# Moving router tables, a first transposition and a gate group within one core's instruction order (decoder layer with mixture of experts, Trainium2)

## The reference, cut to what matters

```
x = x + attention(layernorm(x))                       # 16 heads of 16
x = x + mlstm(q=layernorm(x), k=v=ctx, gates)         # 8 heads of 32
x = x + moe(layernorm(x))                             # 8 experts, 2 taken per token

# gates of the mlstm, for all tokens
pre  = 15 * tanh((concat(q, k, v) @ ifgate_w.T + b) / 15)
lf   = cumsum(log_sigmoid(f_pre)); running maximum m; d = exp(...)
den  = max(|sum|, exp(-m)) + 5e-5
# router
probs = softmax(x @ router_w + router_b); top 2 of 8
out  += weight(e) * (gelu(x @ up[e].T) @ down[e].T)   # for each chosen e
```

## Time and profile before

| what | value |
|---|---|
| time, median of 3 runs | 1005.02 us (1004.59 to 1009.46) |
| the profiled execution: its own time | 1006.74 us |
| its span, first to last instruction | 1005.0 us |
| what lies around the span | 1.74 us |
| PE, DVE, ACT, POOL busy | 89%, 61%, 48%, 52% |
| mean granted TensorE clock | 0.947 of full |
| second stage, about | 339 to 571 us |
| overlap of second and third stage, about | 571 to 640 us |
| tiles alone, about | 640 to 1003 us |

### The profile page before, as it was taken

The page is one execution under the profiler, slowest core; times in us unless marked ns, Lnnn a source line. Parts: engine busy times, 40 slices in busy tenths (PEclk is TensorE's granted clock), DMA queues, the critical chain, the costliest instruction groups (busy, mean ns, idle before and its releaser), DMA issues.

```text
span 1005.0 us, 31744 instructions
## 1 busy us (share of the span) xinstructions
PE 894.1 (89%) x11966; PEld 662.6 (66%) x11966; DVE 614.9 (61%) x1340; ACT 484.4 (48%) x810; POOL 526.7 (52%) x660
## 2 busy tenths in 40 slices
PE   4798898989897777789989798999999999999995
PEld 3566666766665445566666486787787878787783
DVE  4766767777666434777778657555555555555553
ACT  3556766766666445555555444233333333333331
POOL 2545655655655333467878767644434443444342
PEclk8999999999998778798989789999999999999998
DMA  9112343234234654245555324343333332333322
GB/s 282 55 26 73 79 105 114 76 86 135 77 85 128 134 155 139 86 143 172 173 169 174 111 61 91 78 92 49 49 50 50 50 49 46 53 46 53 50 29 27
DMA packets 133198, 92.97 MB, mean 93 GB/s; under 512 B 75712, under 2 KB 114112, under 8 KB 132928
## 3 DMA queue, kind: packets, MB, share of 16 engines
q1 hardware_dynamic: 119760, 73.10, 26.5%
q0 software_dynamic: 13296, 17.83, 10.7%
HBM read 54.65 MB, written 37.32 MB: 92 GB/s over the span
## 4 chain that ended last, share of the span: by engine, by line
PE 59%; DVE 12%; ACT 7%; POOL 6%; DMA 5%; issue 4%; SPq 2%; POOLq 0%; DVEq 0%; ACTq 0%
PE pair L950 19%; PE pair L964 11%; PE pair L966 6%; POOL sm L1567 3%; PE pair L679 3%; PE pair L665 3%; PE pair L643 3%; DMA o_scr<-On 2%; PE pair L692 2%; DMA STG<-wup_in 2%; PE pair L821 1%; PE pair L916 1%; DVE SD L1146 1%; ACT xn L1319 1%; PE pair L835 1%
## 5 line engine op out<-in xcount | busy, mean ns | idle before, releaser
L950 PE MATMUL pair<-XTs,WU 128*128 128x128 bf16 x3408 | 287.2, 221 | 10.2 <-DVE XTs L1287 4.5
L950 PEld LDWEIGHTS pair<-XTs,WU 128*128 x3408 | 240.9, 99 | 77.8 <-issue 15.0
L1604 POOL DMA_INDIRECT out_d<-XB x71 | 115.4, 1626 | 208.4 <-DVE XB L1309 178.9
L964 PE MATMUL pair<-WD,Hh 128*128 x568 | 215.5, 380 | 0.0
L1480 ACT ACTIVATE Hf<-pair 128x512 f32<-128x512 f32 x142 | 84.9, 598 | 227.1 <-PE pair L950 227.1
L1300 DVE CAST Hh<-Hf 128x512 bf16<-128x512 f32 x142 | 63.0, 444 | 173.1 <-ACT Hf L1480 171.7
L966 PE MATMUL pair<-WD,Hl 128*128 x568 | 155.1, 273 | 0.0
L1525 POOL TENSOR_SCALAR_AFFINE_SELECT PT<-PT 128x512 f32<-128x512 f32 (+1 forms) x96 | 74.7, 792 | 61.4 <-ACT PT L1338 55.2
L1302 DVE TENSOR_TENSOR Hl<-Hf,Hh 128x512 bf16<-128x512 f32 x142 | 99.8, 703 | 4.9
L1036 DVE TENSOR_REDUCE mxn<-pair 128x4 f32<-128x1024 f32 x64 | 75.2, 1216 | 25.9 <-PE pair L624 25.9
L1146 DVE TENSOR_TENSOR SD<-pair,SD 128x1024 f32<-128x1024 f32 x48 | 58.6, 1221 | 40.8 <-ACT SD L1422 33.3
(11 more groups left out here) (241 smaller groups left out, 1807.7 us busy)
## 6 DMA issues: line engine op xcount, KB each, us to landing
XB<-xs_scr SPq DMA_DIRECT2D x71, 130.0 KB, 2.1
STG<-wup_in SPq DMA_DIRECT2D x32, 256.0 KB, 4.9
q_scr<-SPL SPq DMA_DIRECT2D x16, 512.0 KB, 4.0
STG<-wdn_in SPq DMA_DIRECT2D x32, 256.0 KB, 2.9
o_scr<-On SPq DMA_DIRECT2D x32, 128.0 KB, 4.1
Mm<-o_scr SPq DMA_DIRECT2D x16, 256.0 KB, 3.0
CnT<-ctxt_in SPq DMA_DIRECT2D x16, 256.0 KB, 4.7
CX<-ctx_in SPq DMA_DIRECT2D x16, 256.0 KB, 4.0
```

The lines of the kernel that those rows point to most:

```text
L950: t = e.matmul(upb(j, k)[:, 128 * (fm % 4):128 * (fm % 4) + 128], WU[:, bass.ds(reg[j] * 4096 + off, 128)], XTs[:, r, hx, dk, :], start=n ...
L964: e.matmul(yb[r][:, 0:512], Hh[:, r, hsl], WD[:, bass.ds(reg[i] * 4096 + 512 * fk, 512)], start=fk == 0, stop=False, skip_group_check=True)
L1604: e.indirect_dma_start(out=out, out_offset=bass.IndirectOffsetOnAxis(ap=XS[:, i % NX, 256:257].bitcast(I32), axis=0), in_=Yf[:, i % NY, :] ...
```

## The change

Three things are done, all in the order of steps. No instruction is added or dropped on any engine.

First, in `rest`, GE of the second gate group goes from (4, 0) to (4, 2), Gp from (4, 1) to (5, 0) and Go from (4, 2) to (5, 1).

Second, in `tail`, part -1 is taken out of the first block of five and put ahead of the last PV (batch 15, unit 2); parts 0 to 3 stay where they are.

Third, around the last pair's router steps: R2 comes after part 40 (before: 41), R3 after part 41 (before: 41), R4 after part 46 (before: 44), R5 and R6 after part 50 (before: 48). The tables no longer follow R6 in one piece: they are cut in three, after parts 52, 54 and 56. The whole overlap gets four more parts.

```
-            (3, 0): (("GA", z), ("Gt", 1)), (3, 1): (("GT", 1),), (3, 2): (("Gs", 1),), (4, 0): (("GE", 1),), (4, 1): (("Gp", 1),),
-            (4, 2): (("Go", 1),)}
+            (3, 0): (("GA", z), ("Gt", 1)), (3, 1): (("GT", 1),), (3, 2): (("Gs", 1),), (4, 2): (("GE", 1),), (5, 0): (("Gp", 1),),
+            (5, 1): (("Go", 1),)}
...
-    tail = (("PV", z, 1), ("B4x", a), ("R6", z - 4), ("PV", z, 2), ("B3", z), ("B4o", a), ("B5s", a), ("B5", z - 2), ("experts", 5),
+    tail = (("PV", z, 1), ("B4x", a), ("R6", z - 4), ("experts", 1), ("PV", z, 2), ("B3", z), ("B4o", a), ("B5s", a), ("B5", z - 2), ("experts", 4),
...
-            ("B6", z), ("experts", 4), ("R1", z), ("experts", 6), ("R2", z), ("R3", z), ("experts", 3), ("R4", z), ("experts", 4),
-            ("R5", z), ("R6", z), ("tables", 0), ("experts", 17))
+            ("B6", z), ("experts", 4), ("R1", z), ("experts", 5), ("R2", z), ("experts", 1), ("R3", z), ("experts", 5),
+            ("R4", z), ("experts", 4), ("R5", z), ("R6", z), ("experts", 2), ("tables", 0), ("experts", 2), ("tables", 1), ("experts", 2),
+            ("tables", 2), ("experts", 13))
...
+        def vector_tables(e, w, link, n):
+            if n == 0:      # L1261 to L1269 of before
...
+            elif n == 1:    # L1270 to L1276
...
+            else:           # L1277 to L1281
```

More of the change, by code:

```diff
@@ L1221, in vector_mlstm @@
                 elif kind == "tables":
-                    vector_tables(e, w, link)
+                    vector_tables(e, w, link, b)
                 elif kind == "R6":
@@ new lines, in vector_tables @@
+        def vector_tables(e, w, link, n):
+            if n == 0:
+                e.tensor_copy(cni[:, :], CNT).then_inc(t_ci, 1)
+                link(e.tensor_tensor(t8[:, 1, :], CNT, CF[:, C_RB:C_RB + 8], ALU.subtract))
+                e.tensor_copy(t8[:, 5, :], PMe[:, :])
+                link(e.tensor_scalar(t8i[:, :], t8[:, 1, :], 63.5, 1.0 / 128.0, ALU.add, ALU.mult))
+                e.tensor_copy(t8[:, 2, :], t8i[:, :])
+                link(e.tensor_tensor(t8[:, 5, 1:8], PMe[:, 1:8], PMe[:, 0:7], ALU.subtract))
+                e.tensor_scalar(t8[:, 6, :], t8[:, 5, :], -128.0, None, ALU.mult)
+                link(e.tensor_tensor(t8[:, 2, :], t8[:, 2, :], t8[:, 5, :], ALU.subtract))
+                e.scalar_tensor_tensor(t8[:, 6, 0:7], t8[:, 5, 1:8], 128.0, t8[:, 6, 0:7], ALU.mult, ALU.add)
+            elif n == 1:
+                e.tensor_tensor_scan(t8[:, 4, :], t8[:, 2, :], t8[:, 2, :], 0.0, ALU.add, ALU.max)
+                link(e.tensor_scalar(t8[:, 3, :], t8[:, 2, :], -128.0, float(REG), ALU.mult, ALU.add))
+                e.tensor_scalar(t8[:, 7, :], t8[:, 5, :], 128.0, None, ALU.mult)
+                link(e.tensor_tensor(te8[:, :, :], over(t8[:, 4, :], NF), tile_nos(0, NF), ALU.is_le))
+                e.tensor_tensor(t8[:, 3, :], t8[:, 3, :], t8[:, 6, :], ALU.add)
+                link(e.tensor_reduce(TE[:, :], te8[:, :, :], AX.X, ALU.add))
+                e.tensor_scalar(TE[:, :], TE[:, :], 7.0, None, ALU.min)
+            else:
+                link(e.tensor_tensor(te8[:, :, :], te8[:, :, :], over(t8[:, 3, :], NF), ALU.mult))
+                e.tensor_copy(TEi[:, :], TE[:, :])
+                link(e.tensor_reduce(RB[:, :], te8[:, :, :], AX.X, ALU.add))
+                link(e.scalar_tensor_tensor(RB[:, :], CF[:, C_J:C_J + NF], 128.0, RB[:, :], ALU.mult, ALU.add))
+                e.tensor_scalar(RBi[:, :], RB[:, :], t8[:, 7, 0:1], None, ALU.add).then_inc(t_rb, 1)
```

22 lines of the change are left out of this document (removed).

## The result

The changed kernel took 1001.41 us (median of 7 runs, 1000.63 to 1004.4), the kernel before in the same comparison 1007.1 us (median of 7, which include the three of the table above). The ratio is 0.9947, 95% interval 0.9927 to 0.9966: 0.5% faster, within what I had forecast (1000.2 us, range 996.9 to 1003.6). The profiled execution took 1000.63 us with a span of 998.9 us, against 1006.74 and 1005.0.

A forecast was written before the change was run, and what follows sets the result against it. PE was taken as the bound, busy 89% of the span. The three edits, -0.4 + 1.1 + 4.1 = 4.8 us, came off the 1005.0 us median for 1000.2 us, range 996.9 to 1003.6.

The forecast's parts named there:

- First edit, -0.4 us: Gate group moved: PE's 3 us lead ends waiting for R3's result; 0.4 us lost, bounds 1.5 us either way.
- the replay: Forecast's step-by-step timing of the new order; at the gate group, the product of (5, 1) starts at 428.9, against 428.83.
- 0.4 us loss: Price put on a possible slow clock behind PE's new gap of nearly 2 us ahead of the scores of (5, 2).
- Gp takes the lead back: Gate group on DVE: Gp's 3.0 us ahead of the product of (5, 1) uses up batch 3's power coming about 3 us sooner.
- Second edit, +1.1 us: Part -1 ahead of the last PV: part 0 starts at 574.7 instead of 575.80; 1.1 us gained, bounds 0.3 to 2.8.
- the bound on the clock: Parts 0 to 3: an earlier start may end the slow clock stretch sooner, for up to 1.7 us more.
- rival C: Gate group gains what its gap promises, or slow stretch after part 0 ends sooner: 1.5 or 1.7 us more; chance 0.2.
- Third edit, +4.1 us: Router steps and tables: wait moves from part 56 to 64, which starts at 633.85 against 637.94; bounds 1.8 to 5.4 us.
- rival B: Clock falls in the gap ahead of part 64 or at (5, 2): 3.0 us gained, 1002.0 us; chance 0.28.
- Rival D: Table work and Gp on DVE held up beside POOL: four steps hit lose 2.4 us, 1002.6 us; chance 0.07.
- this stays: Ahead of part 0, PE still needs 1.29 us after low(0) for the register load and what follows it.
- its 1.3 us is exposed: At part 64 the register load, unseen before, stands behind the wait for low(8) and now costs 1.3 us.

The follow-up runs named there:

- e10: The change with Gp and Go both at (5, 2), behind the product of (5, 1): 1012.11 us, ratio to before 0.9935.
- e1: The kernel before with only the gate group (GE, Gp, Go) moved to its new places: 1010.67 us, ratio to before 1.0019.
- e3: The kernel before with only the last pair's router steps and the three table pieces placed as in the change: 1006.22 us, ratio 0.9979.
- e5: The change itself, measured again in a later comparison: 1014.86 us, ratio to before 0.9972.
- e2: The kernel before with only part -1 put ahead of the last PV: 1005.57 us, ratio to before 0.9963.
- e4: The change with the gate group back in its old places: 998.24 us, ratio to before 0.9911.
- e6: The change with the second and third table pieces each a tile later: 1015.97 us, ratio to before 0.9976.
- e7: The change with the load of the expert numbers put ahead of PE's wait for low(j): 1008.80 us, ratio to before 0.9902.
- e9: The kernel before with only the load of the expert numbers put ahead of PE's wait: 1014.97 us, ratio to before 0.9962.

## Why the prediction was right, and where it was not

The time forecast, 4.8 us saved, met the 5.3 us of the ratio (0.53% of 1007), but two of its terms were wrong by 2 to 4 us in opposite directions. That the sum fits is luck as much as insight: the interval of the ratio alone allows 3.4 to 7.4 us. By its own steps:

**First edit, -0.4 us.** The chain on DVE held: no wait at L757 (0.6 us in the forecast), 1.99 us of idle time ahead of the scores of (5, 2), the product of (5, 1) at P + 24.1 us where the replay had P + 24.8, because B4x came 0.7 us sooner than replayed. R4 followed 0.6 us sooner instead of at the same time. What was too small is the price of the clock behind the gap, "0.4 us loss": the lower level lasted 10 us, in all five kernels with this order, which turned the 0.6 us into 0.8 us lost at P + 51 us. The term comes out near its 0.4 because the two misses oppose each other. The argument that Gp takes the lead back is what e10 tested: with Gp behind the product, the gap and the slow stretch are gone and P to R is 3.5 us shorter.

**Second edit, +1.1 us.** The step itself was exact: V to U is 1.2 us shorter, and from the end of low(0) to part 0 it took 575.24 - 574.02 = 1.22 us (1.29 in the forecast). What failed is the bound on the clock: "an earlier start may end that stretch sooner, for up to 1.7 us more" was half of rival C at a chance of 0.2. It came in every kernel with the second edit, and beside before, e1 and e3 it is worth 3.4 to 4.8 us. I had priced the slow stretch by parts 0 to 3 alone, the 24 matmuls of the earlier trace rows and one row, and never looked for its end. The rows of before that I had not read show it at 0.50 from 576 to 587 us. At half speed over 11 us that is a much larger stake than 2.74 us of matmuls. Why the stretch ends sooner with this edit stays open.

**Third edit, +4.1 us.** The wait moved from part 56 to part 64, with the register load inside, as written: forecast 2.5 to 2.9 us, measured 2.54. From part 48 to 64 it took 14.24 us against 13.75 in my replay. DVE came to the tables 0.3 us later than replayed and needed 0.5 us more for them and the steps between, about what four instructions cost that ran long (0.54, 0.43, 0.67 and 0.77 us, where 0.17, 0.16 or 0.23, 0.42 and 0.69 are usual; by their starts it is some 0.6 us); the exposed load took 1.0 us instead of 1.3. Then the clock fell: rival B, at 0.28. "Gaps of 1.8 us left it, 3.1 and 3.8 us lost it; 2.7 lies between" took the length of the gap as what decides, and e5 shows that it does not: its clock stayed up behind 2.52 us in the same kernel. Tile 8 took 6.94 instead of 5.57 us, 1.4 given back (1.8 forecast). From T2 to T10 the edit brought 2.1 us against before, 2.3 by rival B, and more against e1 and e2 (58.1 and 59.3 us).

**Rival D** was named for two-input steps. Those of the tables ran at their usual 0.61 and 0.17 us in after. Of the four that ran long three have one input, and POOL was at work beside them. The Trainium skill, SBUF — State Buffer, section "Who interferes with whom", says of copies, casts and tensor_scalar that they too can enter a mode that contends with GpSimd. The rows above agree with that part of the rule. The part that the forecast had drawn on, two inputs in SBUF, shows outside of the steps that the edits move: L1212 in after and L1214 in before, two-input steps of R3, each took 1.10 us beside a subtraction of 1.15 us on POOL. Gp's four subtractions ran as long as before. So the rival's mechanism is real, and its price in the moved steps was under 1 us.

**What was in neither.** The 3.2 us lost from R to V come with a larger share of the lower clock level, 0.86 against 0.89, which e2 has as well and e4 has not. 1.4 of them stand directly behind the gap of the gate group, as above; of the other 1.8 I cannot say that they belong to the change. So after's -6.1 us of span is 4.9 from the second edit with its clock, 2.1 from the third, 0.6 from the first, 1.9 from before any change, less 3.2 from R to V and 0.3 at the end.

**The load at every eighth tile.** The forecast took the exposed load as given ("this stays"; "its 1.3 us is exposed"). It was the cheapest thing to mend, one line moved, and worth 4.5 to 6.6 us by the medians, more than the first edit or the third.

## What to carry to other kernels

Where an engine's pause is followed by a slow clock, read the clock rows to the end of the slow stretch before pricing the pause: here an edit that started part 0 1.2 us sooner brought another 3.4 to 4.8 us of clock. And do not price the clock by the length of a gap alone: the same gap of 2.5 us lost it in one execution and left it in the next, and a gap of 2 us that the change itself made was followed by 10 slow microseconds. Where a wait of one engine is removed by moving steps, follow all the steps that move with it: the DVE work beside the transposes took back what PE had gained, until it too was put behind the product that the others wait for. And look at what stands behind the same wait without needing it; a register load moved ahead of it brought most for the least.

## What the runs showed of the hardware

- How long PE's clock stays at the lower level (0.50) while PE is busy did not follow from the gap ahead of it: 11 us behind 3.09 us (before, e1, e3, part 0), 10 us behind 1.99 us (after, e1, e5, e6, e7, scores of (5, 2)), some 3 us behind 3.7 to 3.9 us (before, e1, e2, e9, part 56), and 3 us or nothing behind 2.1 us (after and e4, part 0).
- Behind 2.54 and 2.52 us ahead of part 64, the same kernel lost the full level once (after) and kept it once (e5).
- The mean clock over 134 to 137 us of the second stage lay between 0.86 and 0.92 in before, after and e1 to e4, which have the same order there; PE was busy for 120.0 to 125.8 us with the same work.
- A DVE instruction with two SBUF inputs and only 4 elements a partition took 1.10 us instead of 0.17 beside a POOL subtraction of 1.15 us (after, L1212).
- In the second and third group ACT stood 0.9 to 5.6 us for a releaser outside of what the profile shows, three to seven times per execution between 380 and 680 us, and the kernel before was 1% slower than beside the first group. What it waits for stays open.
- The loads of eight registers took 842 to 912 ns (least and median) where they stood behind the wait and 591 to 606 ns where they stood ahead of it (after and e7, tiles 16 on). Those of tiles 0 and 8, from the early table, took 607 to 779 ns in both places. The Trainium skill, DMA: Bandwidth & Descriptors, section "Latency and other measured facts", gives a floor of about 600 ns for such a load, with which the second pair agrees.
